# Moving the moments behind the second clip, and the low parts of staged rows behind the fourth, on VectorE

## The reference, cut to what matters

```python
x = x + attention(layernorm(x), ctx_1024, ...)
# attention: lat = layer_norm(x)*g+b, ctx = layer_norm(context)*g+b
#   q = lat @ Wq; k, v = split(ctx @ Wkv); k = rope(k, cos, sin)
#   attn = softmax(clip(q k^T / 8, -11, 11)); out = (attn v) @ Wo + bo
x = x + experts(layernorm(x), ...)      # one shared expert, two of eight routed ones
```

## Time and profile before

| | |
|---|---|
| time, median of 3 runs | 2223.13 us (2220.79 to 2226.14) |
| the profiled execution | 2221.47 us |
| its span, first to last instruction | 2219.8 us |
| granted TensorE clock, mean | 0.995 |
| busy: PE, PEld, DVE, ACT, POOL | 97%, 71%, 81%, 61%, 13% |
| PE idle for a clip (L871), PEld idle for a clip | 9.3 us in 15 waits, 35.7 us in 41 |
| one batch of the loop (slots 0 to 7) | 187.5 us |

### The profile page before, as it was taken

How to read it: one execution, slowest core, us unless ns; L and a number is a source line. 1 busy time by engine, 2 the same in 40 slices (tenths; PEclk the granted TensorE clock), 3 DMA queues, 4 the chain that set the end, 5 groups by cost and what they waited for, 6 DMA issues and landing times. The chain is left out here.

```text
span 2219.8 us, 48796 instructions
## 1 busy us (share of the span) xinstructions
PE 2157.2 (97%) x18002; PEld 1579.6 (71%) x18002; DVE 1799.5 (81%) x2416; ACT 1351.4 (61%) x1914; POOL 293.9 (13%) x300
## 2 busy tenths in 40 slices
PE   6999999999999999999999999999997999999998
PEld 5666666666666666666666666655886999999997
DVE  7999989899899988989989998897534555557777
ACT  6675676567567566656756755564443555567773
POOL 2110000011011000000100100001572121121120
PEclk9999999999999999999999999999998999999999
DMA  7235335334423523533442363132563434336656
GB/s 265 89 116 163 89 111 176 91 95 145 133 86 121 175 80 98 177 102 97 129 145 88 102 197 91 49 110 87 200 227 117 133 129 136 133 126 221 225 186 267
DMA packets 149314, 305.62 MB, mean 138 GB/s; under 512 B 34784, under 2 KB 71776, under 8 KB 146080
## 3 DMA queue, kind: packets, MB, share of 16 engines
q1 hardware_dynamic: 138688, 272.46, 39.2%
q0 software_dynamic: 10176, 30.45, 3.8%
q10 hardware_dynamic: 288, 0.26, 0.0%
HBM read 189.31 MB, written 79.20 MB: 121 GB/s over the span
## 5 line engine op out<-in xcount | busy, mean ns | idle before, releaser
L1030 ACT ACTIVATE probs<-scores 128x1024 f32<-128x1024 f32 x512 | 503.3, 1025 | 331.6 <-PE scores L745 326.3
L871 PE MATMUL sum_ps<-probs,v_nat 128*64 128x512 f32 x2056 | 479.2, 599 | 9.3 <-DVE probs L1229 9.3
L1335 DVE TENSOR_TENSOR sums<-sums,probs 128x1024 f32<-128x1024 f32 x384 | 470.2, 1224 | 12.5
L745 PE MATMUL scores<-q_split,k_split 64*128 64x512 f32 x3072 | 415.5, 395 | 1.8 <-ACT probs L1030 1.8
L1229 DVE TENSOR_SCALAR probs<-probs 128x2048 f32<-128x2048 f32 x256 | 313.1, 1223 | 100.5 <-ACT probs L1030 99.1
L1917 PE MATMUL sum_ps<-down,hid_split 128*128 128x256 f32 x2640 | 353.8, 284 | 7.5 <-DVE acc L2060 3.9
L1917 PEld LDWEIGHTS sum_ps<-down,hid_split 128*128 128x128 f32 x2640 | 341.1, 191 | 26.2 <-issue 7.3
L1894 PE MATMUL scores<-xT,up 128*128 128x512 f32 (+1 forms) x1680 | 348.1, 349 | 0.0
L745 PEld LDWEIGHTS scores<-q_split,k_split 64*128 64x128 f32 x3072 | 282.6, 185 | 57.0 <-ACT probs L1030 5.9
L2051 DVE TENSOR_TENSOR hid_split<-hid,hid_split 128x512 fp32r<-128x512 f32 x205 | 142.1, 693 | 217.9 <-ACT hid_split L1981 217.4
L871 PEld LDWEIGHTS sum_ps<-probs,v_nat 128*64 128x64 f32 x2056 | 134.2, 136 | 240.0 <-issue 188.4
(11 more groups left out here) (228 smaller groups left out, 2186.8 us busy)
## 6 DMA issues: line engine op xcount, KB each, us to landing
k_two<-k_two SPq DMA_DIRECT2D x252, 128.0 KB, 2.3
w_all<-wpack SPq DMA_DIRECT2D x60, 512.0 KB, 4.3
raw<-L_ffn_routed_up SPq DMA_DIRECT2D x27, 1024.0 KB, 5.4
raw<-L_ffn_routed_down SPq DMA_DIRECT2D x27, 1024.0 KB, 5.2
rden<-rden_rows SPq DMA_DIRECT2D x128, 128.0 KB, 2.9
ctx_parts<-stage SPq DMA_DIRECT2D x28, 512.0 KB, 3.4
ctx_all<-ctx_parts SPq DMA_DIRECT2D x14, 1024.0 KB, 7.2
sorted_rows<-zero POOLq DMA_DIRECT2D x64, 162.5 KB, 2.5
```

The costliest lines, as they stand in the source:

```text
L745: last = pe.matmul(scores[j % 2][:, head], k_split[i][own, a, j * P:(j + 1) * P], q_split[i][own, m], start=n == 0, stop=n == 2)
L871: last = pe.matmul(sum_ps[64 * head:64 * head + 64, p % 2], v_nat[p // 2 % 2][:, j, cols:cols + 64], probs[:, j % PROBS, head], start=j == ...
L1030: act.activation(probs[:, j % PROBS], scores[j % 2][:], ACT.Exp, scale=float(HD) ** -0.5).then_inc(s_exp, 1)
L1335: v.tensor_tensor(to, to, probs[:, j % PROBS], ALU.add).then_inc(s_add, 1)
```

## The change

Three steps of `slot` in `vector` swap places; no instruction is added or removed, and the streams of the other engines stay as they are.

```diff
             clip(0)
             add_up(1)
             multiply_out()
-            if p == NORMS - 1 or p < NORMS and not last(b):
-                next_moments()
             if not (last(b) and p == PAIRS - 1):
                 v.wait_ge(s_khi, n + (p + 2))
                 low_k((p + 1) % 2)
...
             clip(2)
+            if p == NORMS - 1 or p < NORMS and not last(b):
+                next_moments()
             add_up(2)
             add_up(3)
-            low_stages()
             if has(b, p, "k"):
                 v.wait_ge(s_projout, act_before(b, p, 1))
                 v.wait_ge(s_klo, n + (p + 2))
...
             clip(4)
             if p == NORMS - 1 or p < NORMS and not last(b):
                 norm_shift(p, result_norm(b) if p == NORMS - 1 else b * NORMS + (p + 1))
+            low_stages()
             add_up(4)
             add_up(5)
```

## The result

| | before | changed |
|---|---|---|
| median on the same chip | 2222.14 us (4 runs) | 2255.01 us (4 runs, 2251.12 to 2258.16) |
| ratio, 95% interval | | 1.0141 [1.0127, 1.0155] |
| profiled execution, span | 2221.47, 2219.8 us | 2253.48, 2251.8 us |
| one batch, mean of 0 to 6 | 187.8 us | 192.1 us |

What follows compares the result with a forecast made beforehand. The prediction took VectorE from clip(2) of slot 3 to clip(0) of slot 5 as the bound. Terms of 1.10, 1.23 and 1.71 make 4.04 us a batch, 28.3 in seven, plus 0.5: +28.8, 2252 us, range 2234 to 2261.

Steps and rivals of the forecast that it cites:

- Paid in full: Work added to VectorE between clip(2) of slot 3 and clip(0) of slot 5 lengthens the time by its whole length.
- two signs of being wrong: Gaps at the keys staying at 0.81 us, or VectorE idle between clip(2) of slot 3 and slot 5.
- 1.83 us later: Slot 3: moments (1.95 us) leave the gap before clip(2), delaying everything behind by 1.95 - 0.12 us.
- The refund: Moments between clip and addition save 0.12 us, since independent instructions start 1.13 us after a clip, dependent additions 1.26.
- End of slot 1, 1.10 us: VectorE 1.19 us late at out_part, which frees the PSUM bank for the next keys; 0.09 room leaves 1.10.
- of slot 2, 1.23: End of slot 2: VectorE 1.83 us late at out_part, 0.60 room, so the next keys come 1.23 us later.
- Slots 3 to 5, 1.71: Per batch, slot 3's delay of 1.83 us less slot 4's refund of 0.12 reaches TensorE.
- I cost the move at nothing.: Moving low parts and their stores costs 0; if ScalarE's copy waits, up to 1 us a batch, 7 in all.
- Batch 7 and the expert part: Batch 7 adds 0.5 us, since only slot 4 has moments there; the expert part stays as long as before.
- The last clips gain: Rival: earlier clip(2) and clip(4) remove waits of 0.16 and 0.89 us, 7.4 us faster, 2216; chance 0.05.
- No change: Rival: VectorE's idle time in slots 0 to 3 and 7 absorbs the lateness, about 2222; chance 0.06.
- The delays carry further: Rival: slot 1's lateness, stores or slot 6's context wait each add 3 to 7 us or more, 2262 to 2270; chance 0.06.

Runs made afterwards that it cites:

- all three variants of that group: Kernel before with slot 3's low parts ahead of clip(2), 0.9976; slots 3 and 4's moments earlier, 0.9973; both plus slot 4's low parts ahead of clip(2), 0.9943.

## Why the prediction was right, point by point

- **Bound.** Right in kind: the kernel waits for VectorE from `clip(2)` of slot 3 to `clip(0)` of slot 5, and taking work out of it made all three variants of that group faster. "Paid in full" holds for work that is added; of 1.2, 1.95 and 3.15 us taken out, 0.83, 0.88 and 2.05 arrived, and idle time before `clip(2)` of slot 4 took most of the rest. Wrong in size: "So TensorE loses 0.16 + 0.55 + 0.89 + 1.49 = 3.1 us a batch" counted idle time of the weight loads as lost. The matmuls' own row, already on the page before, has 9.3 us, 1.3 a batch. With every one of these gaps gone, slots 3 to 5 were 1.75 us shorter. The forecast did not rest on this sum, only on growth of the gaps. Neither of the two signs of being wrong came: the gaps at the keys grew, and VectorE has no idle time between `clip(2)` of slot 3 and slot 5.
- **Moments in slot 3, "1.83 us later".** Right: the idle time before the clip grew by 1.93, and from clip to addition it now takes 1091.34 - 1088.18 = 3.16 us against 1.26, 1.90 later.
- **The refund.** From a clip to the independent instruction behind it 1089.32 - 1088.18 = 1.14 us, to a dependent addition 1.26. It stands as 0.12, and over the changed kernel's attention all 36 clips with moments right behind them have 1.13 to 1.14, all 66 with an addition right behind 1.25 to 1.26. But the moments' last step hands over to the addition after 0.17 us, where `low_k` used to follow it after 0.10, so only 0.05 of the 0.12 was left in slot 3. By the Trainium skill's rule in "VectorE: DVE Perf Modes", "Rules for kernel authors", the two distances would be equal, and the trace does not agree; no run here isolates the refund's effect on the total.
- **End of slot 1, 1.10 us, and of slot 2, 1.23.** Measured 1.14 and 1.11. (The gap at slot 2's keys was forecast as about 1.6 us; with the term of 1.10 on top of 0.81 it should have been 1.9, and 1.98 was measured.) The experiment with `out_part` ahead removes both.
- **Slots 3 to 5, 1.71.** Measured 0.48 + 0.86 + 0.45 = 1.79. But the profile listed other gaps than "about 1.1, 2.0, 0.29 and 2.5": 1.15, 2.20, gone, 2.20. The sum held since the delay behind is one delay, wherever TensorE takes it.
- **"I cost the move at nothing."** The step that failed, twice, with opposite signs. Its gain was ruled out because `clip(0)` of slot 5 stands behind the same work of VectorE. That holds only while VectorE has no idle time in the stretch. With the moments moved alone it has 0.76 us in slot 4, and the low parts' move in slot 3 removes it: 0.44% in the ratios, of which the two profiled executions (spans of 2256.6 and 2251.8 us) show half. The forecast of 1.71 was right only with the second part in. Its cost was looked for at ScalarE's refill of the block, and the list of waits has no such wait; alone, the move costs 0.2%, on SyncE's queue, through the two 4 KB round trips, to the context of slot 6.
- **The gap at slot 6's keys.** The sum had no term for it, and it grew by 0.46 us a batch, 3.2 of the 32. 28.8 and 3.2 make 32, and part of that agreement is luck: 1.11 for 1.23, 1.79 for 1.71 and 1.14 for 1.10 cancel. How much of the 3.2 the stores cause is open, see below.
- **Batch 7 and the expert part.** +0.7 and +0.3 us, against 0.5 and nothing; the program's start, 0.5 us shorter, hid the difference.
- **Rivals.** "The last clips gain" failed as stated: `clip(2)` of slot 3 was bound by its exponential. "No change" leaned on TensorE's 97%. The Trainium skill ("Perfetto Trace Analysis", "Identifying the Most-Contended Engine") says to optimize the engine of highest occupancy first, but to go by the weight loads' busy share for TensorE and not by the matmuls'. By that, VectorE's 81% stands above PEld's 71%, and the runs agree: every edit here, down to 0.9943, was to the order on VectorE or SyncE. "The delays carry further" was partly true: the item of the context did happen, at the low end of its price.

**What stays open.** With slot 4's stores in their old place, but the moments moved, `den_rows` still took 2.3 to 4.5 us, with the context's first half as far ahead of it as before in six of seven batches. Slot 4's stores, issued at the same time in the slot, landed 1.0 to 2.1 us later there than in the kernel before in six of seven batches, so transfers were slower already; the runs do not say what shares the DMA engines with them. How the 3.2 us divide between the stores' move and the moments' is not settled: in single profiles the mean gap was 1.52 us with the moments alone, 2.06 with those of slots 3 and 4, 1.75 with slot 4's low parts left in place, and 1.86 in the changed kernel. With slot 4's moments in slot 3 and no low part moved it was 4.63 us in one batch and 1.2 to 2.1 in the others.

## What to carry to other kernels

A step that fills a wait for another engine is free where it stands; before moving it, look for the idle time in front of the instruction that it is moved behind, and take what remains there as the price. Count a delay at the next place where another engine takes something back (a PSUM bank, a buffer), not only at the clip or sum that the profile names. When a step is moved, follow its DMA down the issuing queue to the next small transfer that is waited for.

## What the hardware showed

- **Idle weight loads are not idle TensorE.** A wait that shows 1.04 us before a load showed 0.16 before the matmul (2.35 and 1.47 at another), so the first 0.88 us cost nothing there.
- **A small write behind a large load.** The 4 KB round trip took 1.64 us with nothing ahead, 2.0 to 2.6 (4.1 in one batch) with 1 MB issued 3.0 to 3.3 us ahead of it, 2.9 to 4.0 in the changed kernel, where it is issued 2.5 to 2.8 us ahead (1.4 in one batch), and 5.0 to 6.1 with it 1.1 to 1.65 us ahead and the second of two 512 KB stores landed 1.1 to 1.8 us ahead. The distance is not all of it: with 3.0 to 3.3 us ahead and the moments moved it took 2.3 to 4.5.
- **Two large loads close together.** Each half of the context (1 MB) landed 5.8 to 7.8 us after its issue when sent 6 to 8 us apart (kernel before and changed kernel); sent 1.2 us apart, the second took 8.7 to 9.7.
- **Independent work behind a clip** starts 0.12 us sooner than dependent work (1.14 and 1.26 us).
